# A two-layer decoder on one core: the maximum of channel attention's scores before the output addition, later loads held behind its weights, and two reorderings in grouped attention

## What is computed

```python
x = x + channel_attention(layernorm(x))       # L0_attn
x = x + cross_attention(layernorm(x), ctx)    # L0_xattn, 32 heads of 8
x = x + quantised_linear(layernorm(x))        # L0_ffn
x = x + linear_attention(layernorm(x))        # L1_attn, 16 heads of 16
x = x + gated_convolution(ctx, layernorm(x))  # L1_xattn
x = x + grouped_attention_and_moe(layernorm(x))  # L1_ffn: 16 query heads, 4 key/value heads of 128, 8 experts
```

```python
q, k, v = xn @ Wq, xn @ Wk, xn @ Wv
w = softmax(q.T @ k / sqrt(8), axis=-1)       # 256 x 256: channels attend to channels
y = (w @ v.T).T @ Wo
```

## Time and profile before

| | us |
|---|---|
| median of 3 runs (1364.26 to 1366.4) | 1364.35 |
| the profiled execution, its own time | 1367.16 |
| its span, first to last instruction | 1364.7 |
| TensorE busy | 1186.6 (87%) |
| VectorE busy | 765.1 (56%) |
| POOL busy | 603.6 (44%) |
| ScalarE busy | 577.8 (42%) |

### The profile page before, as it was taken

One profiled execution on the slowest core, in us unless ns is written; L12 is line 12 of the kernel. 1 busy time (PEld: TensorE's weight loads), 2 busy tenths in 40 slices (PEclk: granted clock), 3 DMA queues, 4 the chain that ended last, 5 costly groups with the idle time before them and its releaser, 6 DMA issues. The chain is left out here.

```text
span 1364.7 us, 24627 instructions
## 1 busy us (share of the span) xinstructions
PE 1186.6 (87%) x7421; PEld 832.2 (61%) x7422; DVE 765.1 (56%) x1930; ACT 577.8 (42%) x1504; POOL 603.6 (44%) x752
## 2 busy tenths in 40 slices
PE   4888588885899969978999999999999859999995
PEld 3666355563555534436878888878888626665663
DVE  2444368875788857984566666666666532222221
ACT  1333266663333320004666566666566413333331
POOL 1000245552555536745666556666565312233222
PEclk9999699997999989988999999999999869999998
DMA  6000000000699204014000000000000312322223
GB/s 249 1 0 0 12 12 13 15 12 2 152 206 206 58 1 160 0 40 210 1 9 17 16 13 12 15 12 15 15 13 13 147 35 39 46 46 43 43 44 85
DMA packets 46353, 69.40 MB, mean 51 GB/s; under 512 B 4736, under 2 KB 42672, under 8 KB 45232
## 3 DMA queue, kind: packets, MB, share of 16 engines
q1 hardware_dynamic: 36864, 52.69, 14.5%
q0 software_dynamic: 7152, 9.34, 4.2%
q10 hardware_dynamic: 2272, 6.56, 1.3%
HBM read 57.12 MB, written 32.58 MB: 66 GB/s over the span
## 5 line engine op out<-in xcount | busy, mean ns | idle before, releaser
L1717 PE MATMUL ga.pkq<-ga.xnT,g.early 128*128 128x128 f32 x1280 | 156.7, 276 | 1.0 <-ACT ga.halves L1636 1.0
L1717 PEld LDWEIGHTS ga.pkq<-ga.xnT,g.early 128*128 128x128 f32 x1280 | 151.4, 193 | 9.6 <-issue 8.2
L1761 PE MATMUL ga.turn_out<-g.early,ga.aT 128*128 128x256 f32 x512 | 119.1, 386 | 10.8 <-ACT ga.aT L1658 10.8
L1498 POOL TENSOR_TENSOR ga.halves<-ga.halves,g.ga_sinT 128x512 f32<-128x512 f32 x80 | 104.3, 1304 | 50.9 <-ACT ga.halves L1636 50.9
L1761 PEld LDWEIGHTS ga.turn_out<-g.early,ga.aT 128*128 128x128 f32 x512 | 95.5, 191 | 25.6 <-issue 8.8
L1506 POOL TENSOR_TENSOR ga.kqT<-ga.by_cos,ga.halves 128x512 f32<-128x512 f32 x80 | 101.7, 1272 | 16.5 <-issue 16.5
L1551 DVE TENSOR_TENSOR ga.by_cos<-ga.pkq,g.ga_cosT 128x512 f32<-128x512 f32 x80 | 55.3, 691 | 95.6 <-PE ga.pkq L1717 51.5
L1643 ACT ACTIVATE ga.e<-ga.psc,ga.negmax 128x128 f32<-128x128 f32 x256 | 90.4, 366 | 40.6 <-DVE ga.negmax L1564 39.7
L1872 DVE TENSOR_TENSOR ex.hidden<-ex.silu,ex.p 128x512 f32<-128x512 f32 x39 | 26.8, 688 | 124.8 <-PE ex.p L1925 118.4
L1742 PE MATMUL ga.paT<-ga.pT,ga.v 128*128 128x512 f32 x128 | 68.7, 619 | 13.9 <-ACT ga.pT L1651 10.0
L1920 PE MATMUL ex.p<-g.spare,ex.xnT 128*128 x156 | 76.9, 616 | 1.1 <-ACT ex.xnT L1900 0.8
(11 more groups left out here) (288 smaller groups left out, 2634.2 us busy)
## 6 DMA issues: line engine op xcount, KB each, us to landing
mo_rows<-in_pad_rows SPq DMA_DIRECT2D x1, 18447.0 KB, 99.6
ex.row<-mo_rows SPq DMA_DIRECT2D x39, 129.0 KB, 2.1
g.spare<-in_mo_w SPq DMA_DIRECT2D x1, 4096.0 KB, 12.3
g.late<-in_mo_w SPq DMA_DIRECT2D x1, 4096.0 KB, 22.7
g.early<-in_mo_w SPq DMA_DIRECT2D x1, 4096.0 KB, 12.6
g.ctxT<-in_ctxR SPq DMA_DIRECT2D x1, 2048.0 KB, 12.7
xa.ctxT<-in_ctxT SPq DMA_DIRECT2D x16, 128.0 KB, 2.5
g.spare<-cv_rows SPq DMA_DIRECT2D x1, 2048.0 KB, 7.7
```

The lines of the kernel that those rows point to most:

```text
L1498: nc.gpsimd.tensor_tensor(by_sin[:, par, :].rearrange("p (h t) -> p h t", h=REP), halves[:, par, :].rearrange("p (h t) -> p h t", h=REP), ...
L1717: last = nc.tensor.matmul(pkq[:, par, j * P:(j + 1) * P], w[:, q, at * P:(at + 1) * P], xnT[:, s.par, q, :], start=(q == 0), stop=(q == C ...
L1761: last = nc.tensor.matmul(pout, aT[:, h // REP, (h % REP) * P:(h % REP + 1) * P], g.ga_wo[:, h, :], start=(h == 0), stop=(h == H - 1))
```

## The change

Four things are changed.

1. **Loads.** Two `x` parts stay in `load_first`; SP issues wk between them. ACT issues identity, wq, wv and wo. There is a semaphore for query and key weights, one for wv and one for wo, and each is waited for at the first use: TensorE ahead of the first `pqk` and the first `pv`, VectorE ahead of the first scaling of wo. Batches 4 to 15 of `x` and all loads of other stages are issued by SP after it has seen wo landed. POOL casts the identity in step 2 of the first stage.
2. **Channel attention, VectorE.** The maximum of the scores of s-1 comes first, and then the addition of s-2.
3. **Semaphores.** POOL clears those of cross attention and the quantised linear (23, 2 and 11, so 36) in step 2 of linear attention. There are two more global semaphores.
4. **Grouped attention.** ScalarE's `copy_aT(b, 3)` stands between `swap(s, 3)` and `swap(s, 4)`. TensorE's transposes of the next input stand in r = 2 instead of r = 3.

```diff
 def load_first(nc, g, h):
...
         @block.sync
         def _(sp):
-            for k in range(len(X_PARTS) - 1):
-                part = slice(X_PARTS[k], X_PARTS[k + 1])
-                sp.dma_start(g.x[:, part, :], h["x"][:, part, :]).then_inc(g.x_loaded[k], 16)
+            load_x(g, sp, 0)
+            sp.dma_start(g.ca_wqk[:, :, D:2 * D], h["ca_wk"]).then_inc(g.ca_qk_loaded, 16)
+            load_x(g, sp, 1)
 
         @block.scalar
         def _(act):
             act.dma_start(g.ident[:], h["ident"]).then_inc(g.ident_loaded, 16)
-            act.dma_start(g.ca_wqk[:, :, 0:D], h["ca_wq"]).then_inc(g.ca_loaded, 16)
-            act.dma_start(g.ca_wqk[:, :, D:2 * D], h["ca_wk"]).then_inc(g.ca_loaded, 16)
-            act.dma_start(g.ca_wv, h["ca_wv"]).then_inc(g.ca_loaded, 16)
-            act.dma_start(g.ca_wo, h["ca_wo"]).then_inc(g.ca_loaded, 16)
+            act.dma_start(g.ca_wqk[:, :, 0:D], h["ca_wq"]).then_inc(g.ca_qk_loaded, 16)
+            act.dma_start(g.ca_wv, h["ca_wv"]).then_inc(g.ca_v_loaded, 16)
+            act.dma_start(g.ca_wo, h["ca_wo"]).then_inc(g.ca_o_loaded, 16)
 
         @block.gpsimd
         def _(pool):
             nc.gpsimd.memset(g.minus_half[:], -0.5).then_inc(g.fill, 1)
-            pool.wait_ge(g.ident_loaded, 16)
-            nc.gpsimd.tensor_copy(g.ident_bf[:], g.ident[:]).then_inc(g.fill, 1)
...
@@ channel attention, SP
+            sp.wait_ge(g.ca_o_loaded, 16)
+            load_x(g, sp, 2)
             sp.dma_start(g.quad[:], h["quad"]).then_inc(g.consts_loaded, 16)
...
@@ channel attention, POOL, in step
                 if s.base is None and s.n == 2:
+                    pool.wait_ge(g.ident_loaded, 16)
+                    nc.gpsimd.tensor_copy(g.ident_bf[:], g.ident[:]).then_inc(g.fill, 1)
...
@@ channel attention, VectorE, in step
-                b = s.back(2)
-                if b.on:
-                    dve.wait_ge(out_done, upto(b))
-                    nc.vector.tensor_tensor(g.x[:, b.i, :], pout[:, 0:D], g.x[:, b.i, :], ALU.add).then_inc(x_added, 1)
                 b = s.back(1)
                 if b.on:
                     dve.wait_ge(scores_done, upto(b))
...
                     nc.vector.tensor_scalar(negmax[:, b.par, :], negmax[:, b.par, :], -scale, None,
                                             ALU.mult).then_inc(max_ready, 1)
+                b = s.back(2)
+                if b.on:
+                    dve.wait_ge(out_done, upto(b))
+                    nc.vector.tensor_tensor(g.x[:, b.i, :], pout[:, 0:D], g.x[:, b.i, :], ALU.add).then_inc(x_added, 1)
...
+                    if b.base is None and b.n == 0:
+                        dve.wait_ge(g.ca_o_loaded, 16)
...
@@ channel attention, TensorE
-            pe.wait_ge(g.ca_loaded, 16 * g.ca_loads)
...
+                    if s.base is None and s.n == 0:
+                        pe.wait_ge(g.ca_qk_loaded, 32)
...
+                    if s.base is None and s.n == 0:
+                        pe.wait_ge(g.ca_v_loaded, 16)
...
@@ linear attention, POOL, in step
+                if s.base is None and s.n == 2:
+                    for sem in g.finished_next:
+                        nc.gpsimd.sem_clear(sem)
...
@@ grouped attention, ScalarE, in step
                 if s.on:
                     swap(s, 3)
+                if b.on:
+                    copy_aT(b, 3)
+                if s.on:
                     swap(s, 4)
-                if b.on:
-                    copy_aT(b, 3)
...
@@ grouped attention, TensorE, in step
-                    if r == KV - 1 and n.on:
+                    if r == 2 and n.on:
                         pe.wait_ge(xn_ready, upto(n))
```

More of the change, by code:

```diff
@@ L196, in allocate @@
     g.filt_loaded = m.sem("filt_loaded")
-    (g.ident_loaded, g.consts_loaded, g.ca_loaded, g.xa_loaded, g.la_loaded, g.ctx_loaded, g.ga_loaded,
+    (g.ident_loaded, g.consts_loaded, g.ca_qk_loaded, g.ca_v_loaded, g.ca_o_loaded, g.xa_loaded, g.la_loaded, g.ctx_loaded, g.ga_loaded,
      g.mo_loaded, g.fill, g.pads_stored) = map(m.sem, (
-        "ident_loaded", "consts_loaded", "ca_loaded", "xa_loaded", "la_loaded", "ctx_loaded", "ga_loaded",
+        "ident_loaded", "consts_loaded", "ca_qk_loaded", "ca_v_loaded", "ca_o_loaded", "xa_loaded", "la_loaded", "ctx_loaded", "ga_loaded",
         "mo_loaded", "fill", "pads_stored"))
-    g.const_loads, g.ca_loads, g.xa_loads, g.la_loads = 1, 4, 4, 10
+    g.const_loads, g.xa_loads, g.la_loads = 1, 4, 10
     g.ga_loads, g.mo_loads = 9, 3
@@ L212, in fill_value_windows, with load_x @@
         nc.gpsimd.memset(vd[:, k, :, 0:512].rearrange("p q (g z) -> p q g z", z=32)[:, :, :, 8:16], 1.0)
+def load_x(g, eng, k):
+    part = slice(X_PARTS[k], X_PARTS[k + 1])
+    eng.dma_start(g.x[:, part, :], g.h["x"][:, part, :]).then_inc(g.x_loaded[k], 16)
 def load_first(nc, g, h):
@@ L511, in cross_attention_and_quantised_linear @@
             "xqT_ready", "y_done", "y_added", "w_sum_ready", "wq_ready", "filled"))
+        g.finished_next = m.sems + n.sems
         block = ctx.enter_context(nc.Block())
@@ L1700, in step @@
                     swap(s, 3)
-                    swap(s, 4)
                 if b.on:
                     copy_aT(b, 3)
+                if s.on:
+                    swap(s, 4)
             steps(act, step, 1, 4)
```

## The result

The changed kernel takes **1328.85 us** (median of 6 runs, 1325.82 to 1330.82). The kernel before, run beside it on the same chip, took 1366.88 (1364.26 to 1369.21), a little more than in the runs shown above. The ratio is 0.9716, with a 95% interval of 0.9697 to 0.9736: faster by 2.8%. Of 1366.88 that is 38.8 us; the two medians are 38.0 apart. The forecast was 34.7 less, and 1329.6. The profiled execution took 1330.82 with a span of 1328.8, so its span is 35.9 shorter than that of before.

The account below looks back on a forecast made before the run. TensorE, busiest almost everywhere, idles for weights at the start, scaled Wo in channel attention and the fourth aT in grouped attention. Savings 9.7 + 12.6 + 1.3 + 1.1 + 10.0 = 34.7 take 1364.35 to 1329.6 us, range 1323 to 1340.

Parts of the forecast that it names:

- loads, to the first `pmix`: Kernel start: TensorE waits for its input only, no longer for all four weights; 9.7 us less, ends 8.2 and 10.0.
- loop, first to last `pmix`, less the last step: Channel attention steps: maximum first removes the 11.6 us wait for scaled Wo, plus overlap; 12.6 us, ends 11.6 and 13.6.
- last step: End of channel attention: `pmix` can come at 135.21 instead of 136.50; 1.3 us less.
- clock of the last step, last `pmix` to the stage's end: End of channel attention: after a shorter gap the last `pmix` runs at full clock; 1.1 us less, ends 0 and 2.2.
- grouped attention: Output projection no longer waits for the fourth `aT`, transposes give 0; 10.0 us less, ends 8.5 and 10.8.
- other stages: Following stages: a shifted start can move their low-clock pipeline fills by an estimated 3 us either way.
- One bound: Kernel start: all four weights with batches 1 to 3 of `x`, 1.6 MB, take at most 9.7 us by packets.
- The rival built on this slack: Channel attention: chain stretched by 1.0 us uses up 0.4 slack, 7 us come back, about 1337; chance 0.06.
- The wait for `v`: Grouped attention: TensorE comes 0.74 earlier against 0.66 slack, loses perhaps 0.1 in such steps; at most 2 us in profile.
- The clears: Linear attention, step 2: POOL's 36 semaphore clears, up to 2.5 us once, cost 0, at worst 2.5.
- the signs that I named: Profile after: transposes at 5.7, load waits within 0.5, steps 6.5 without scaled-Wo wait, stage end near 118, `aT` wait near zero.
- the signs of being wrong: First `pqk` waiting for weights beyond 8 us, or a wait over 0.3 us per step at L442 or L1735.

Follow-up runs that it names:

- the control: The changed kernel once more, unaltered, profiled a second time: 1327.95 us.
- e1: The kernel before with only the loads part of the change (without the clears): ratio 0.9928.
- e9: Changed kernel, POOL's value-window fills in step -1, ScalarE's grouped-attention copies reordered around swap(s, 1), second aT ahead of the r = 3 exponentials: 1333.17 us, ratio 0.9745.
- e5: Changed kernel, but SP issues batches 4 to 15 of x behind batches 1 to 3, without waiting for wo: 1328.5 us, ratio 0.9721.
- e7: Changed kernel with the reduction to the maximum done twice in each step of channel attention: 1337.66 us, ratio 0.9783.
- e3: The kernel before with only ScalarE's copy of the fourth aT put between the two swaps in grouped attention: ratio 0.9904.
- e4: The kernel before with only the transposes of the next input moved from r = 3 to r = 2 in grouped attention: ratio 0.997.
- e2: The kernel before with only the maximum put ahead of the addition in channel attention: ratio 0.9885.
- e8: Changed kernel with ScalarE's copies of the second pT and first aT ahead of swap(s, 1) in grouped attention: 1332.45 us, ratio 0.9746.
- e12: Changed kernel with extra, unread TensorE matmuls in gaps of the last channel attention steps and early cross attention: 1326.7 us, ratio 0.9702.

## Why the prediction was right, and where not

By its own steps, with the first profile pair:

| term | forecast | measured |
|---|---|---|
| loads, to the first `pmix` | 9.7 | 9.0 (25.80 to 16.83); 10.3 with the control (15.46); 10.6 in e1 (15.23) |
| loop, first to last `pmix`, less the last step | 12.6 | 14.6 |
| last step | 1.3 | 1.3 (3.31 to 2.02) |
| clock of the last step, last `pmix` to the stage's end | 1.1 | 0.4 (6.65 to 6.25) |
| grouped attention | 10.0 | 12.8 over 12 steps, 15.9 in all |
| other stages | 0, 3 either way | -5.2 |

- **Loads: right, for a reason that is half right.** In the first profile the query and key weights came 0.5 us later than the need that I had worked out; in the control, e1 and e9 they were there in time (`pqk` at 6.68). The gain of 9.0 to 10.6 brackets my 9.7. But that large rows of `x` crowd out the weights was not what cost the time once each weight was waited for at its first use: with that, and wk on SP's queue, holding `x` back brought nothing that can be measured (e5). One bound was added up wrongly: wo with all that goes ahead is 1408 packets (768, 512 of wv and wo, 128 of batches 1 to 3), 11.4 us at 149 per us and not 9.7; wo landed at 8.8, by 2.45 + 6.3, so nothing hung on it.
- **The loop: mechanism right, size too small.** The step that was mis-sized is the overlap: I took half of 14 x 0.14. A step gained 1.12 (7.40 to 6.28), 0.83 of it from the idle column and 0.29 from groups that now follow closely. e7 shows the same loss in reverse, and 0.14 to 0.22 us of slack against the 0.4 that I named. The rival built on this slack would have cost more than I gave it: a stretch of 1.0 over a slack of 0.4 leaves 0.6 and not 0.5 a step, and over the true slack 0.8.
- **The clock's term failed.** The last `pmix` took 3.66 us instead of the 1.99 forecast, more than the 3.12 of before; only `pout` behind it was shorter, 1.13 against 2.07. The 0.4 that is left is no gain of the change: kernels with the old order took 6.2 to 6.3 from this `pmix` to the stage's end in e1, e3 and e4. I had argued from a gap of 2.46 after which a matmul ran at full speed. One such row says nothing on the next gap: behind the same gap of 2.02 the last `pmix` took 2.00 in e2, 2.64 in e5, 3.05 in e8 and 3.66 here. In e2, where it fell out well, the stage's end gave 2.1. With the gap filled it took 1.89 (e12).
- **Grouped attention: mechanism right, size too small.** I counted the idle column (10.8) and no overlap, though I had counted one in channel attention: the copy alone gave 0.97 per step where the column has 0.77 (9.2 in 12 waits). The transposes were costed at 0. Alone they gave 1.4, probably for what stood behind them in r = 3; with the copy moved ahead, as in the change, eleven steps of twelve show the 0. One step of before, 29.78 where its neighbours have 29.0, adds 0.7 to the 12.8, and the 3.1 outside the twelve steps are within what executions differ by. The wait for `v` came as foretold, 0.8 us in the stretch of 370 us; a single one of 2.9 outside it makes the stage's total 3.7, over the 2 that I had allowed.
- **The clears cost nothing.** Step 2 of linear attention in the changed kernel's timeline, as in the earlier trace rows:

```profile
331.50 2.99 POOL L882 TENSOR_TENSOR la.norm<-la.msq,g.minus_half 128x16 f32<-128x16 f32 x1 [1.64 <-DVE la.msq L930]
...
335.69 0.41 DVE L952 TENSOR_TENSOR la.un<-la.u,la.norm 128x256 f32<-128x256 f32 x1
```

  POOL's power operation starts 0.30 us behind VectorE's last `msq` (331.20), against 0.25 before, and its reader starts 4.19 us behind it, against 4.24. The 36 clears fit into the idle time.
- **Given back elsewhere: 5.2 us**, more than the 3 that I allowed. In cross attention it is the dip of the granted clock. For the 1.6 in linear attention and convolution the second profile, with 0, points to a difference between executions too; that was not tried by itself.

The loop and grouped attention gave 7.9 us more than forecast; the loads, the clock of the last step and the other stages 6.6 less. That the total, 34.7 against 35.9, was closer than its parts is luck: terms too small and terms too large made up for each other. So is it that the time was met to 0.8 us: the kernel before had been at 1364.35 when I forecast, and was at 1366.88 beside the changed one. Against that the saving was 3 to 4 us larger than forecast.

Of the signs that I named, the first transposes, the stage's end (117.9), and no wait of `pmix` for the scaled Wo from the third step on came true; the wait for a load was 1.09 us in the first profile, over the 0.5 that I gave, and the steps were 6.28 instead of 6.5. None of the signs of being wrong came.

## What to carry to other kernels

Where an engine is the bound and waits once in each step, take the idle column as the low end: a group that no longer waits also runs into the tail of the one before, 0.2 to 0.3 us a step here. In an in-order queue cost what stands behind a moved instruction, not only its own input; a copy may go ahead of an instruction that is itself still waiting, but a swap that feeds another engine moves that engine's work too, and may make it collide. And where a pipeline fills or drains, count on 2 to 4 us that differ between executions, and take a second profile of the same kernel before you explain them. Filling TensorE's gaps held the clock here; what it saved was not clear of the noise.

## What was not expected of the hardware

- Thirty-one extra matmuls held the clock: with the gaps filled, it stayed at a granted 1.00 for the whole fill of cross attention, even across a later gap of 3.09 us, and the kernel was no slower for them (1326.7 against 1328.85 us, intervals that overlap).
- A VectorE operation of 0.17 us takes up to 1.28 us beside a POOL operation, and in e9, where it took 0.74 on average, the steps alternate between 27.98 and 29.45 us.
- Why cross attention falls into one of two lengths 3 us apart, and why the changed kernel showed the longer one in both profiles, stays open.
